# A two-layer graph network on one core: one-hot counting rows read from PSUM, one PSUM bank for a group's sums, and a register load on TensorE after every tile

## What is computed

```python
# layer 0 (feat = x)
t1 = feat @ W1
msg = t1[src] + feat[src] * feat[dst] @ W2
msg = msg / (sqrt(out_deg[src]) * sqrt(out_deg[dst]))[:, None]
agg = segment_sum(msg, dst)
embed = leaky_relu(where(in_cnt > 0, t1 + agg, 0) + b); embed /= norm(embed)
x = layernorm(x + embed)
# layer 1
xt = x @ W.T + b
out = segment_sum(xt[src], dst) / (in_deg + 1)[:, None]
x = layernorm(x + out)
```

## Time and profile before

| | |
|---|---|
| median of 3 runs | 4266.98 us (4265.9 to 4276.45) |
| profiled execution, own time | 4292.12 us |
| its span, first to last instruction | 4290.4 us |
| mean granted TensorE clock | 0.595 of full speed |
| busy: PE / PEld / DVE / ACT / POOL | 84% / 74% / 37% / 9% / 73% |
| DMA | 489.92 MB, mean 114 GB/s |

### The profile page before, as it was taken

How to read it: one execution, slowest core, us unless ns; L and a number is a source line. 1 busy time by engine, 2 the same in 40 slices (tenths; PEclk the granted TensorE clock), 3 DMA queues, 4 the chain that set the end, 5 groups by cost and what they waited for, 6 DMA issues and landing times.

```text
span 4290.4 us, 60042 instructions
## 1 busy us (share of the span) xinstructions
PE 3621.7 (84%) x17483; PEld 3168.4 (74%) x17483; DVE 1600.2 (37%) x4104; ACT 381.6 (9%) x1359; POOL 3140.3 (73%) x3175
## 2 busy tenths in 40 slices
PE   6578888888888888888887888888888888888888
PEld 5477777877777777777776777777777777767776
DVE  9954444444444444444442222222222222222222
ACT  8800000000000000000000000000000000000000
POOL 2277777777777777777776777777777777777776
PEclk8755656666566656666565555555555555555555
DMA  5243333333333333343433344343343433434433
GB/s 164 87 129 115 111 115 113 112 115 110 115 110 116 111 114 115 110 115 109 116 109 98 112 117 117 112 116 113 116 117 112 117 114 114 118 111 117 117 113 104
DMA packets 236973, 489.92 MB, mean 114 GB/s; under 512 B 57537, under 2 KB 136916, under 8 KB 236948
## 3 DMA queue, kind: packets, MB, share of 16 engines
q0 software_dynamic: 150944, 409.95, 33.6%
q1 hardware_dynamic: 86004, 79.66, 5.8%
HBM read 450.84 MB, written 38.54 MB: 114 GB/s over the span
## 4 chain that ended last, share of the span: by engine, by line
POOL 69%; issue 25%; DVE 3%; PE 2%; POOLq 1%; DMA 0%; DVEq 0%; SPq 0%; ACT 0%; ACTq 0%
POOL ring L408 68%; DVE hot L598 2%; PE banks L1034 1%; POOL r_edge L416 1%; POOLq L444 0%; POOL ring L412 0%; PE banks L940 0%; POOLq L405 0%; PE banks L1013 0%; POOLq L406 0%; DVEq L590 0%; DVEq L640 0%; DMA ring<-in_dst 0%; PE banks L999 0%; DMA ring<-scaled_x,idx 0%
## 5 line engine op out<-in xcount | busy, mean ns | idle before, releaser
L1034 PE MATMUL banks<-dst_hot,ring 128*128 128x64 f32 x12544 | 2949.5, 395 | 562.5 <-DMA ring<-x,idx 250.8
L1034 PEld LDWEIGHTS banks<-dst_hot,ring 128*128 128x128 f32 x12544 | 2576.2, 294 | 938.3 <-DMA ring<-x,idx 377.0
L408 POOL DMA_INDIRECT ring<-x,idx x1563 | 1525.4, 976 | 499.2 <-issue 476.2
L408 POOL DMA_INDIRECT ring<-scaled_x,idx x1535 | 1539.4, 1003 | 467.9 <-issue 467.3
L743 DVE TENSOR_TENSOR big<-banks,big 128x128 f32 x784 | 228.7, 292 | 1936.8 <-PE banks L1034 1934.7
L715 DVE TENSOR_TENSOR dst_hot<-win_iota,dst_rel 128x256 f32<-128x256 f32 x787 | 337.0, 428 | 311.1 <-issue 310.9
L523 ACT COPY idx<-src_col 128x8 int32 (+1 forms) x392 | 77.5, 198 | 2875.4 <-PE banks L1034 2875.3
L940 PE MATMUL banks<-hot 128*128 128x98 bf16 x2848 | 210.7, 241 | 47.9 <-DVE hot L598 47.1
L940 PEld LDWEIGHTS banks<-hot 128*128 128x128 bf16 x2848 | 194.1, 120 | 67.6 <-DVE hot L598 44.8
L1013 PE MATMUL banks<-wt_s,a_t 128*128 128x256 f32 x392 | 179.0, 637 | 1.3 <-ACT a_t L537 1.3
L598 DVE TENSOR_TENSOR hot<-ring,count_to 128x2048 bf16<-128x2048 bf16 (+1 forms) x160 | 162.0, 1094 | 0.2
(11 more groups left out here) (118 smaller groups left out, 1043.4 us busy)
## 6 DMA issues: line engine op xcount, KB each, us to landing
ring<-x,idx POOLq DMA_INDIRECT x1563, 2.8
ring<-scaled_x,idx POOLq DMA_INDIRECT x1535, 2.8
x<-out_t SPq DMA_DIRECT2D x98, 128.0 KB
x_t<-x SPq DMA_DIRECT2D x98, 128.0 KB, 2.2
big<-in_x SPq DMA_DIRECT2D x1, 12416.0 KB
x_t<-in_x SPq DMA_DIRECT2D x97, 128.0 KB, 2.2
result<-out_t SPq DMA_DIRECT2D x97, 128.0 KB
scaled_x<-big SPq DMA_DIRECT2D x6, 1792.0 KB, 13.8
```

What stands on the lines that cost most here:

```text
L408: g.indirect_dma_start(ring[:, u, :], None, table[layer], bass.IndirectOffsetOnAxis(ap=idx[:, u:u + 1], axis=0)).then_inc(rows_in[u], 16)
L1034: last = nc.tensor.matmul(group_sum(k % 2)[:, f, :], ring[:, u, f * P:(f + 1) * P], dst_hot[:, k % HOTS, j, :], start=j == 0, stop=j == GT ...
```

## The change

Three things are changed.

1. A row of counting numbers is copied once into PSUM bank 3 for each of the two one-hots of the layer loop, and `group_hot` and the destinations' `hot_batch` read it from there. The copy of `count_to` becomes fp32, since the PSUM tensor is. The source one-hots before the layer loop still read `count_to` in SBUF.
2. A group's sums take one bank (columns 0 to 127 of bank 0 or 1) and not two. The start mark stands only on the first matmul of the group and the stop mark only on the last.
3. After each tile TensorE loads element 0 of `base_row` into a register, which nothing uses (`pace`).

```diff
         def group_sum(buf):
-            return banks[:, 2 * buf:2 * buf + 2, 0:WIN]
+            return banks[:, buf, 0:KF * WIN].rearrange("p (k n) -> p k n", k=KF)
 
         hist = banks[:, 4, 0:HI]
+        win_count = banks[:, 3, 0:WIN]
+        bin_count = banks[:, 3, WIN:WIN + PAIR * P].rearrange("p (c a) -> p c a", a=PAIR)
...
+            bins = [count_to[:, :, :], bin_count]
+
             def hot_batch(n, batch, half, which):
...
                     last = nc.vector.tensor_tensor(hots[half], vals.unsqueeze(2).to_broadcast(shape),
-                                                   count_to[:, 0:size, :].unsqueeze(1).to_broadcast(shape), ALU.is_equal)
+                                                   bins[which][:, 0:size, :].unsqueeze(1).to_broadcast(shape), ALU.is_equal)
...
             nc.vector.tensor_copy(dst_rel[:, TILES:TILES + AHEAD * GT], dst_rel[:, 0:AHEAD * GT])
+            nc.vector.tensor_copy(win_count, win_iota[:, :])
+            nc.vector.tensor_copy(bin_count, count_to[:, :, :])
             ordered()
...
                 last = nc.vector.tensor_tensor(dst_hot[:, buf, :, :],
-                                               win_iota[:, :].unsqueeze(1).to_broadcast([P, GT, WIN]),
+                                               win_count.unsqueeze(1).to_broadcast([P, GT, WIN]),
                                                rel, ALU.is_equal)
...
+            def pace():
+
+                pe.value_load(base_row[0:1, 0:1], min_val=0, max_val=NPAD)
+
...
                         for f in range(KF):
                             last = nc.tensor.matmul(group_sum(k % 2)[:, f, :], ring[:, u, f * P:(f + 1) * P],
-                                                    dst_hot[:, k % HOTS, j, :], start=j == 0, stop=j == GT - 1)
+                                                    dst_hot[:, k % HOTS, j, :], start=j == 0 and f == 0,
+                                                    stop=j == GT - 1 and f == KF - 1)
                         last.then_inc(tiles_done, 1)
+                        pace()
```

## The result

The changed kernel takes 4164.55 us (median of 4 runs, 4162.99 to 4167.06) against 4269.35 us for the kernel before in the same comparison: ratio 0.9753 [0.9736, 0.977], 105 us less. Its profiled execution took 4167.06 us, that of the kernel before 4292.12 us, 125 us less. The forecast was 4157 us.

A forecast was written before the change was run, and what follows sets the result against it. POOL's gathers with their issue pauses were taken as the bound. The profiled 4292.1 us less 112 us of stretch plus 2 for the load gave 4182, and 4157 from the runs' median, 25 us lower; range 4135 to 4285 us.

The forecast's parts named there:

- The mechanism: POOL's gathers are stretched beside DVE operations with two SBUF inputs, 124.8 us in all; one input in PSUM ends it.
- So I leave a tenth: Stretch left by unchanged DVE operations with two SBUF inputs: a tenth of 124.8 us, so 112 us saved (100 to 125).
- The median of the runs is 25 us below that execution; a gain of 110 us on it: Last step of the sum: the profiled execution's gain, 110 us, taken from the runs' median to give 4157 us.
- The 2 us for the layer ends: Cost of the load where PE runs each layer's last six tiles alone: some 1 us each, 2 us.
- The price on DVE: `hot_batch` with a PSUM input slows to 2.3 and 1.8 us, 3.8 us more a round, hidden at no cost.
- The load on PE: Register load after each tile: 0.93 us a tile, 38.2 us a round in layer 0 against POOL's 40.3, so hidden.
- I take 0.305 us: Duration assumed for PE's load, from DVE's loads in the loop, with PE's one row of 1.094 us as other end.
- 0.38 us behind a load: Estimated time on PE's sequencer after each load, for two bounds instructions and the pauses.
- 0.24 us: Time for PE's sequencer to hand out a tile's 8 records before the load, at most.
- A: Rival: PE's load is slow and PE becomes the bound, 4,570 us (load 0.6) or 6,150 (1.1); chance 0.10 each.
- B: Rival: PE narrowly becomes the bound in layer 0 only, about 4,200 us, or 4,225 at 1.04 us a tile; chance 0.13.
- C: Rival: POOL still stands behind `hot_batch`, only layer 1 gains, 4,230 to 4,290 us; chance 0.07.

The follow-up runs named there:

- d2: c1 with the counting row of `hot_batch` as fp32 in SBUF instead of PSUM: 4347.16 us, ratio 1.0186 to the kernel before.
- c1: The changed kernel without the register load on PE, on a usual chip: 4169.41 us, ratio 0.9766 to the kernel before.
- e3: The changed kernel with the bias row of layer 1 also read from PSUM bank 2, on a pausing chip: 5151.96 us against 5044.88 for the kernel before.
- a1: The changed kernel without the register load, on a chip with pausing sequencers: 5112.16 us against 5100.22 for the kernel before, ratio 1.0025.
- a2: The kernel before with the register load alone added, on a chip with pausing sequencers: 5186.83 us against 5100.22, ratio 1.0179.
- d3: The kernel before with the register load alone added, on a usual chip: 4256.89 us, ratio 0.9977 to the kernel before.

## Why the prediction was right

**The mechanism** was right, and d2 shows it. The Trainium skill (SBUF — State Buffer, section Who interferes with whom) has the same rule, two SBUF inputs of a DVE instruction against a GpSimd instruction that reads SBUF. The traces agree, at 1067 and 953 ns a gather with 2.3 us operations in both. They show also that an indirect DMA issued by GpSimd counts as such a reader.

**"So I leave a tenth"** of the stretch, 12 us, was the right size: the changed kernel's profiled execution keeps 10.3 us by its own median gather, and c1's keeps 14.5. The gathers at lines 778 and 813 are instances.

**"The median of the runs is 25 us below that execution; a gain of 110 us on it"** is the term that was mis-sized. The gain was worked out on the profiled execution and taken whole from the median of other runs. But the profiled execution is no typical one. Its plain gather was 3 ns longer, which is 9 us, and the rest of the 25 us must be stretch that the timed runs do not have. An estimate from the table: the rest of 1224.5 to 1227.3 us and 3098 x 0.946 = 2930.7 us of plain gathers make a floor of 4155 to 4158 us, if the timed runs had such gathers (they have no trace). The runs at 4269 us then held 111 to 114 us of stretch, not 125, and those at 4165 us hold 7 to 9. The gain was 105 us where the prediction had 110. This is 5 of the 8 us by which the forecast was too low; the other 2.4 us are the median it started from, 4266.98 us against 4269.35 in the result. The 2 us for the layer ends don't show: own time less gathers is 1226.1 us with the loads and 1224.5 without, one execution each, and 1227.3 before. That all of this came to only 8 us is in part luck, since the prediction did not ask what the 25 us were.

**The price on DVE** was right: 2.3 and 1.8 us foreseen, 2.288 and 1.780 measured, hidden. The Trainium skill (VectorE: DVE Perf Modes, The perf-mode tier table) gives 2293 ns for the first at one element a cycle, and the trace agrees. Its rule spoke against the change, rightly on DVE's time and without effect on the kernel's. In d2 both inputs are in SBUF and one of them is fp32, and it takes 2296 ns: the fp32 row alone is enough to slow the operation, wherever it stands. A bf16 row in PSUM was not tried.

**The load on PE**: "I take 0.305 us" was right (0.301), and leaving 1.094 us aside was sound: it had been taken where the DMA engines were used to 104%, and in the loop, at 41%, the median is 0.301. Whether the DMA load is the reason was not tested. "0.38 us behind a load" and "0.24 us" for handing out were too much. The two bounds instructions last 0.146 and 0.018 us, and a tile costs 0.65 us of sequencer, not 0.93. The 16 weight loads of four tiles took 1.87 us at a granted clock of 1.0, where the prediction's 3.53 us were at 0.5. That is 0.47 us a tile, less than the 0.65 us between loads, so the sequencer must have been ahead of the array there. The error was on the safe side. In layer 0 PE is busy 1714.1 of 1850 us, 0.93, where the prediction had 38.2 of 40.3, 0.95.

**The rivals.** A: the load's median is 0.301 us and the waits for `idx` cost 3.8 us in the whole execution, so it fell. The Trainium skill (DMA: Bandwidth & Descriptors, Latency and other measured facts) has about 600 ns as the floor of such a load; 3136 loads at 0.301 us disagree, and the measurement decides. B fell on the usual chips: POOL waited for `idx` no longer than that in any kernel there. C fell with the gathers of 0.95 us beside `hot_batch`. Where sequencers pause, PE is the bound, and with the load the kernel's stand-in e3 loses 2%. The prediction had no such case: A and B blame the load or the clock, and there PE is the bound even without the load. That the result was taken on a usual chip was luck.

## What to carry to other kernels

An input that is read over and over by a long DVE operation belongs in PSUM when GpSimd issues indirect DMAs beside it and sets the time, even where the operation then takes twice as long (2.29 us for 1.23 here); first see in the timeline that the gathers beside it are stretched and that DVE has room. If the profiled execution lies outside the timed runs, first find out what it has more of (here 9 us of longer plain gathers and some stretch), and work out the floor that lies under both, instead of taking a gain found in one execution from another's median. The register load was hidden here where its sequencer was not the bound, and cost 28 ns a tile at once where it was.

## What was not expected of the hardware

**Chips with pausing sequencers.** The same kernel took 4268 us on some chips and 5045 or 5100 on others, while a gather of layer 0 takes 952 ns in a1 and 953 in c1, the same kernel. What differs is the idle time between instructions, and the longest durations on the sequencers. The rows of a1's matmuls above are an instance; a2's load rows are another (its line's own view; min/median/max):

```profile
L1022 PEldq TENSOR_LOAD <-base_row x3136: 3/301/728, 260.8 to 5175.4; - x196
...
L1022 PEldq SEQ_ASSERT  x3136: 4/18/1421, 261.4 to 5176.0; - x196
```

An instruction of 18 ns lasts up to 1.42 us. What pauses the sequencers stays open; no run separates it.

**The spread of the runs.** The kernel before ran between 4257 and 4278 us over all its timed runs on the usual chips, the changed one between 4163 and 4167. It is tempting to say that with the stretch the spread goes too, but d2 has the most stretch, 190 us, and its five runs lie within 2.7 us (4345.66 to 4348.36). So much stretch does not by itself mean a wide spread. Which gathers start beside which operation may be settled anew in each execution of one kernel and not of another; no run shows it. An instruction whose result nothing uses (d3) moved the time by 11 us.
